# Loading twenty bucket columns into VectorE's registers at once instead of four

## The reference

```
xn = layernorm(x)
h  = xn @ W.T + b;  a1 = h @ w_a1.T + b_a1;  a2 = h @ w_a2.T + b_a2
v  = leaky_relu(a1[row] + a2[col], 0.01)
m  = segment_max(v, row);  ev = exp(v - m[row]);  s = segment_sum(ev, row)
gnn = segment_sum(ev / s[row] * h[col], row)
x  = x + gnn + mix(xn)
x  = x + experts(layernorm(x))       # top 2 of 8, silu(h1) * h3
```

## Time and profile before

| | us |
|---|---|
| median of 3 runs | 3320.83 (3319.59 to 3324.13) |
| profiled execution, whole time | 3308.1 |
| its span | 3306.0 |
| busy: PE, DVE, ACT, POOL | 2443.2, 1739.1, 1227.6, 1141.3 |
| mean granted TensorE clock | 0.859 |

### The profile page before, as it was taken

The page is one execution under the profiler, slowest core; times in us unless marked ns, Lnnn a source line. Parts: engine busy times, 40 slices in busy tenths (PEclk is TensorE's granted clock), DMA queues, the critical chain, the costliest instruction groups (busy, mean ns, idle before and its releaser), DMA issues. The chain is left out here.

```text
span 3306.0 us, 46533 instructions
## 1 busy us (share of the span) xinstructions
PE 2443.2 (74%) x10229; PEld 1689.5 (51%) x10230; DVE 1739.1 (53%) x6232; ACT 1227.6 (37%) x3908; POOL 1141.3 (35%) x1101
## 2 busy tenths in 40 slices
PE   0116888863778778878777787760099999999998
PEld 0113444432556556656555565540067666776765
DVE  7775444434777777777777777771022222222222
ACT  6001222213555555555555555210023332333332
POOL 0000000007666666666666666006511111111111
PEclk9999899875787787786877877985599999999999
DMA  3000111152333333333333336557611211111121
GB/s 141 0 0 32 62 64 64 59 206 72 91 90 90 90 91 90 91 90 90 90 90 91 90 90 85 159 163 234 191 29 30 32 31 31 31 31 32 30 32 26
DMA packets 156692, 258.73 MB, mean 78 GB/s; under 512 B 28097, under 2 KB 109122, under 8 KB 155766
## 3 DMA queue, kind: packets, MB, share of 16 engines
q0 software_dynamic: 62592, 143.11, 18.7%
q1 hardware_dynamic: 93942, 113.93, 10.9%
HBM read 183.18 MB, written 73.75 MB: 78 GB/s over the span
## 5 line engine op out<-in xcount | busy, mean ns | idle before, releaser
L745 POOL DMA_INDIRECT arena<-table,arena x880 | 877.8, 997 | 1180.9 <-DVE arena L826 741.3
L772 PE MATMUL psum<-arena 128*128 128x257 f32 x1760 | 704.2, 533 | 281.4 <-issue 157.8
L772 PEld LDWEIGHTS psum<-arena 128*128 128x128 f32 x1760 | 377.7, 252 | 504.1 <-issue 423.0
L867 DVE SCALAR_TENSOR_TENSOR arena<-arena,psum 128x257 f32 x880 | 423.3, 481 | 351.4 <-remote 249.1
L1262 PE MATMUL psum<-arena 128*128 x1696 | 534.3, 458 | 1.4 <-ACT arena L1337 0.7
L1364 DVE TENSOR_TENSOR arena<-psum,arena 128x341 f32<-128x341 f32 x212 | 109.0, 514 | 641.0 <-ACT arena L1319 454.6
L1395 POOL DMA_INDIRECT out<-arena x106 | 164.7, 1554 | 755.1 <-ACT arena L1345 747.5
L1262 PEld LDWEIGHTS psum<-arena 128*128 128x128 f32 x1696 | 305.7, 190 | 162.3 <-issue 38.1
L795 ACT ACTIVATE arena<-arena 128x128 f32<-128x128 bf16 x880 | 281.0, 390 | 154.5 <-DVE arena L881 108.9
L1295 PE MATMUL psum<-arena 128*128 x1272 | 312.9, 388 | 1.1 <-ACT arena L1327 1.1
L808 ACT ACTIVATE arena<-arena 128x128 f32<-128x128 bf16 x880 | 281.1, 390 | 7.1
(11 more groups left out here) (316 smaller groups left out, 3133.5 us busy)
## 6 DMA issues: line engine op xcount, KB each, us to landing
arena<-table,arena POOLq DMA_INDIRECT x880
expert_in<-arena SPq DMA_DIRECT2D x1, 13674.0 KB
arena<-expert_in SPq DMA_DIRECT2D x106, 129.0 KB, 2.0
mix_inputs<-arena SPq DMA_DIRECT2D x100, 128.0 KB, 1.8
arena<-mix_inputs SPq DMA_DIRECT2D x50, 256.0 KB, 2.9
arena<-xn SPq DMA_DIRECT2D x98, 128.0 KB
arena<-in_w SPq DMA_DIRECT2D x6, 1364.0 KB
out<-arena SPq DMA_DIRECT2D x51, 128.0 KB, 2.2
```

Source lines behind the costliest of these rows:

```text
L745: pool.indirect_dma_start(rows_in[j][:, q * TW:(q + 1) * TW], None, table_d[:, :], bass.IndirectOffsetOnAxis(ap=col_all[:, t:t + 1], axis=0))\
L772: mm(psum[4 + q][:, 0:C + 1], weight[b][:, q * P:(q + 1) * P], rows_in[g][:, q * TW:q * TW + C + 1], start=True, stop=True).then_inc(S("pr ...
L867: v.scalar_tensor_tensor(here, here, alpha[(j - 5) % RING][:, q:q + 1], psum[4 + q][:, 0:C + 1], ALU.mult, ALU.add).then_inc(S("acc_done"), 1)
```

## The change

One load takes the columns of twenty tiles, for five groups (`PER_LOAD`), before the adds of groups 0, 5, 10 and so on. The adds of the four groups after take their columns from the registers that it filled. The 220 loads of four values become 44 loads of twenty.

```diff
+PER_LOAD = 5
...
+            held = []
+
             def step(i, j, k):
                 columns = None
...
                 if live(i, 5):
-                    _, columns = nc.values_load_multi_w_load_instructions(
-                        bt_i[0:1, ds((i - 5) * G, G)], engines=(dve.engine,), min_val=0, max_val=(NT - 1) * TW,
-                        skip_runtime_bounds_check_because="the table holds first columns of buckets")
+                    if (i - 5) % PER_LOAD == 0:
+                        _, held[:] = nc.values_load_multi_w_load_instructions(
+                            bt_i[0:1, ds((i - 5) * G, PER_LOAD * G)], engines=(dve.engine,), min_val=0, max_val=(NT - 1) * TW,
+                            skip_runtime_bounds_check_because="the table holds first columns of buckets")
+                    columns = held[(i - 5) % PER_LOAD * G:(i - 5) % PER_LOAD * G + G]
                 add(i, j, 0, columns)
```

## The result

| | before | changed |
|---|---|---|
| median of 4 runs, us | 3320.56 (3319.59 to 3324.13) | 3372.03 (3367.7 to 3393.57) |
| ratio, 95% interval | | 1.0165 (1.0138 to 1.0192) |
| profiled execution: span, us | 3306.0 | 3365.6 |
| mean granted clock | 0.859 | 0.847 |

The changed kernel is slower by 51.5 us, 59.6 us between the two profiled executions. All of it lies in the gather: the last add starts at 2153.65 us instead of 2092.76, 60.9 us later.

A forecast was written before the change was run, and what follows sets the result against it. The gather's loop of waits was the bound, with TensorE's product releases held back while GpSimd's requests stream. Terms 3.3 + 15 + 0 + 0 = +18 us gave 3326 profiled, 3339 as median; range 3300 to 3390 (own range 3328 to 3355).

The forecast's parts named there:

- the sign of being wrong: Forecast is wrong if the gather stage between first and last add changes by less than 5 or more than 40 us.
- The load: VectorE's register load of twenty values takes 4.5 us, on the line through 302 ns for one and 965 for four.
- rival D: The load's count costs nothing (965 ns for twenty); VectorE wins 93 us before the same stall: 3320 or less; chance 0.06.
- The hole: On VectorE's queue, every fifth group's add starts 3.99 us behind L881; each removed load brings an add 0.53 us forward.
- The reading of the stall: TensorE's releases are held back while gather requests stream, a 2.74 us wait per pair; removed loads lie beside it, worth 0.
- The start: The first load lies on the path to GpSimd's first product wait: +3.3 us, or 0 if count costs nothing.
- The tail: Last eight groups, after the requests end: one long load against seven removed ones, 0, within 3 us either way.
- The collision: GpSimd requests lengthened by an earlier L881 on VectorE: taken as 0, low end -9, high end +31 us.
- step (3): Streaming part: a pair of groups with a load runs 0.7 us over, 42 times: 0 to 30 us, taken as +15.
- Rival B: VectorE becomes the bound, its net loss of 1.42 us per five groups counting in full: +62 us, 3383; chance 0.19.
- Rival A: No difference: GpSimd's stream with its pause sets the pace, pairs with a load pass nothing on: about 3324; chance 0.21.
- C: Faster: the 4 us hole lets held releases through, leaving fewer stalls per five groups: -50 us, 3270; chance 0.12.

The follow-up runs named there:

- one_load_again: Kernel before with one four-value register load for the whole stage instead of 220 (sums in wrong buckets), in a set with the stall: ratio 0.9968.
- single_loads: Kernel before with each column loaded by its own one-value load, placed behind other VectorE work, in a set with the stall: ratio 1.0000.
- long_and_short_3: Kernel before with all 220 loads kept, every fifth taking twenty values instead of four, in a set with the stall: ratio 1.0089.
- after_3: The changed kernel itself, measured again against the kernel before in a set with the stall: ratio 1.0098.
- per4_3: Changed kernel with sixteen-value loads for four groups instead of twenty for five, in a set with the stall: ratio 1.0013 to the kernel before.
- per2: Changed kernel with eight-value loads for two groups instead of twenty for five, in a set without the stall: ratio 1.0080 to the kernel before.
- per4: Changed kernel with sixteen-value loads for four groups instead of twenty for five, in a set without the stall: ratio 1.0093 to the kernel before.
- one_load: Kernel before with one four-value register load for the whole stage (sums in wrong buckets), in a set without the stall: ratio 0.9975.
- before_again: The kernel before, unchanged, run again for its profile in a set with the stall: 3328.8 us.
- lead6: Kernel before with GpSimd waiting for the products of one group later, so requests run one group less ahead, with the stall: ratio 0.9989.

## Why the prediction was right in its direction and too small

Forecast were 18 us, measured 51.5 (59.6 between the profiled executions). The stage from its first to its last add grew by 60 us, beyond the 40 that the prediction itself named as the sign of being wrong.

- **The load**, 4.5 us from two rows: right (4.49). With it fell rival D.
- **The hole**, 3.99 us behind L881, and 0.53 us for each removed load: right (3.96; no wait before the other groups' first adds).
- **The reading of the stall** ("beside the stall, not in it", savings worth 0): right. one_load_again gives 11 of 116 us, single_loads nothing, and long_and_short_3 is within the interval of after_3. The late updates of `product_done` show the stall itself.
- **The start**, +3.3: GpSimd's first product wait went from 3.48 to 6.53 us, +3.05.

```profile
812.38 0.95 POOL L746 DMA_INDIRECT arena<-table,arena  x1 [6.53 <-PE psum L773]
```

- **The tail**, 0 within 3: from the end of the last request to the start of the last group's first add, 28.5 us before and 30.3 after, +1.8.
- **The collision**, 0: right where the prediction was measured (983 and 981 ns per request, and per4_3 shows it absorbed), wrong without the stall, where per2 and per4 pay 23 and 34 us, near its high end of 31.
- **The pair with a load**, step (3), +15 with a high end of 30: this failed. It measured about 59 us, the added pauses less the gaps they replace, 1.4 us for each of the 42 loads. I bounded it by the 0.7 us that the hole stands out over the pair. That holds only while GpSimd keeps its runs of eight ("GpSimd goes on as soon as the products are out, about when it does today"). It doesn't. It stands at the end of its ring, so a product made late by the hole stops it at once (3.56 us at 1031.31, 0.27 us after that product's end), and 79 of its 134 pauses end with such a product, none before. The pause of the next eight requests is then not spared: there are 29 more pauses, and those behind eight are longer, 2.27 us against 1.86. A high end of a whole additional pause per load, 1.9 us, would have been 80 us in all.

Rival B named this ("if late products make GpSimd pause once more per five groups"), and its 3383 was near; 29 more pauses are two for every three loads. But its price, VectorE's net loss of 1.42 us per five groups counted in full, was right by chance: long_and_short_3 has a queue 2.12 us longer per five groups at the same time. Rival A needs the runs of eight whole, and C fewer pauses; there were 29 more. C also took 5.86 us for a group, the mean with the tail; in the streaming part it is 5.93, as the prediction has it further up, and its gain would be 65 us instead of 50.

What stays open: why TensorE's word comes late while gather requests stream, and why it does so in some sets and not in others. No run here took the cause away. The traces of the sets with the stall also record few of the landings of gathers: one_load_again 1487 updates for some 700 requests of sixteen each between 812 and 1860 us, one_load 13199 for some 830. Whether late and missing updates have one cause, the runs don't tell. Nor is it shown why the same program has 44 runs of four in one execution and 76 in another, or what the lower clock level adds after a hole.

## What to carry to other kernels

A register load here costs 0.22 us per value after the first; gathering loads into one instruction saves only 0.08 us for each (302 ns for one value less 221), and makes one hole of many small gaps that other work had partly covered. Before an engine's queue is shortened, ask what ends the wait behind it: here 219 removed loads gained 0.3%, and hiding every load gained nothing. And where a producer stands at the end of a full ring, a stall of its consumer can pass through to it and cost a further pause. With the stall, holes of 3.1 us did not (0.13%) and holes of 4.0 us did (0.5 to 1.65%), so the average slack of the consumer is no bound on the loss.

## What the runs showed that I had not expected

- The same kernel takes 3117 us in some sets and 3317 to 3331 in others. The 200 us are the gather: 5.07 us per group in one_load, 5.99 in one_load_again. A profile from one set shows one of the two.
- In sets with the stall GpSimd's runs are eight requests long in 105 cases of 105 (before_again, one_load_again, single_loads) and in 104 of 104 with one group less ahead (lead6), though VectorE's queue differs by 0.5 us per group.
- The line through one value on TensorE and four on VectorE holds for VectorE alone, within 0.5%: 303 ns for one value (single_loads), 1845 for eight (1849 on the line), 3607 for sixteen (3617), 4488 for twenty (4500). The loads of single_loads, per2 and per4:

```profile
L872 DVEq TENSOR_LOAD <-arena x880: 4/303/722, 803.7 to 2106.9; - x176
```

```profile
L890 DVEq TENSOR_LOAD <-arena x110: 1840/1845/2085, 790.3 to 1919.0; - x110
```

```profile
L890 DVEq TENSOR_LOAD <-arena x55: 3601/3607/3852, 793.9 to 1925.5; - x55
```

- A lengthened request costs nothing in one case and most of its length or more in the other. In per4_3, 36.6 us of longer requests were paid back by 36.0 us of shorter pauses; in per2 and per4, 23 and 34 us of longer requests stand beside 33 and 37 us of time.
